# A decoder layer with a mixture of experts: another split of the last scatters, other load and result orders, paired overflow products and an earlier mask

## What is computed

```python
logits = x @ gate_weight.T;  scores = softmax(logits)
# the 3 best of 8 groups of experts, then the 6 best experts of 64 for every token
pos  = cumsum(one_hot(expert)) * one_hot - 1
slot = expert * C + minimum(pos, C - 1)            # C = 96 slots per expert
buf  = zeros(E * C, H).at[slot].set(x[tok])
out  = silu(buf @ Wg.T) * (buf @ Wu.T) @ Wd.T      # per expert, M = 176
y    = sum(out[slot] * topk_w)
shared = silu(x @ Sg.T) * (x @ Su.T) @ Sd.T
return y + shared
```

## Time and profile before

| what | value |
|---|---|
| median of 3 runs | 699.98 us (697.43 to 700.79) |
| the profiled execution | 692.44 us |
| its span | 690.4 us, mean granted clock 0.987 |
| PE busy | 637.3 us, 92% |
| DVE busy | 471.1 us, 68% |
| POOL busy | 345.6 us, 50% |
| ACT busy | 331.7 us, 48% |
| attention and gate | to about 398 us |
| shared groups 0 to 3, list | 398 to 452 us |
| experts | 452 to 642 us |
| the rest | 642 to 690.4 us |

### The profile page before, as it was taken

The page is one execution under the profiler, slowest core; times in us unless marked ns, Lnnn a source line. Parts: engine busy times, 40 slices in busy tenths (PEclk is TensorE's granted clock), DMA queues, the critical chain, the costliest instruction groups (busy, mean ns, idle before and its releaser), DMA issues. The chain is left out here.

```text
span 690.4 us, 16774 instructions
## 1 busy us (share of the span) xinstructions
PE 637.3 (92%) x6161; PEld 449.1 (65%) x6161; DVE 471.1 (68%) x1278; ACT 331.7 (48%) x630; POOL 345.6 (50%) x381
## 2 busy tenths in 40 slices
PE   3799999999879889999999999999999999999892
PEld 1366666666657667666776455577786778677652
DVE  1477777768779689999896689745554555455656
ACT  2577778777656776777665543122222222222010
POOL 5511322212543345254322346757787777787493
PEclk9999999999999999999999999999999999999997
DMA  8234333355452321432131189159999999944697
GB/s 262 37 64 95 85 62 71 88 110 112 110 118 34 81 68 24 92 81 57 29 103 39 54 220 253 38 142 242 261 259 262 252 247 263 238 77 63 153 356 258
DMA packets 144145, 94.27 MB, mean 137 GB/s; under 512 B 61552, under 2 KB 141680, under 8 KB 144064
## 3 DMA queue, kind: packets, MB, share of 16 engines
q1 hardware_dynamic: 129008, 74.58, 41.3%
q0 software_dynamic: 10400, 14.33, 11.4%
q10 hardware_dynamic: 4656, 4.29, 1.9%
HBM read 60.26 MB, written 24.50 MB: 123 GB/s over the span
## 5 line engine op out<-in xcount | busy, mean ns | idle before, releaser
L1559 POOL DMA_INDIRECT sum_d<-outs,targets x64 | 93.3, 1458 | 27.4 <-issue 14.2
L850 DVE TENSOR_REDUCE mx<-Sc 128x16 f32<-128x1024 f32 x64 | 78.2, 1222 | 27.4 <-PE Sc L455 27.2
L1378 PE MATMUL Sc<-xT,wgu_sb 128*128 128x96 f32 (+1 forms) x768 | 92.8, 271 | 0.0
L1378 PEld LDWEIGHTS Sc<-xT,wgu_sb 128*128 128x128 f32 (+1 forms) x768 | 87.2, 187 | 0.4 <-issue 0.4
L483 PEld LDWEIGHTS O<-vbd,ET 128*64 128x64 f32 x2048 | 66.6, 138 | 28.8 <-issue 16.9
L854 DVE TENSOR_TENSOR E<-Sc,mx 128x1024 f32<-128x1024 f32 x64 | 78.4, 1225 | 6.5
L706 ACT COPY ET<-ring 128x512 f32<-128x512 f32 x128 | 68.9, 590 | 28.1 <-PE ring L467 25.4
L745 ACT ACTIVATE E<-E 128x1024 f32<-128x1024 f32 x64 | 67.7, 1058 | 22.6 <-DVE E L854 22.4
L483 PE MATMUL O<-vbd,ET 128*64 128x34 f32 x2048 | 73.6, 225 | 4.3 <-ACT ET L706 3.8
L467 PE MATMUL ring<-ident,E 128*128 128x128 f32 x512 | 70.7, 280 | 5.6 <-ACT kT L660 5.4
L455 PE MATMUL Sc<-kbd,qT 64*64 64x256 f32 x1024 | 72.0, 384 | 3.8 <-DMA kbd<-kT 3.8
(11 more groups left out here) (212 smaller groups left out, 1210.1 us busy)
## 6 DMA issues: line engine op xcount, KB each, us to landing
wgu_sb<-in_wgu_dram SPq DMA_DIRECT2D x128, 176.0 KB, 3.7
sum_d<-zeros SPq DMA_DIRECT2D x16, 524.0 KB, 5.8
kbd<-kT SPq DMA_DIRECT2D x248, 32.0 KB, 2.2
wgu_sb<-sum_d SPq DMA_DIRECT2D x12, 512.0 KB, 9.3
wda_sb<-in_wd_dram SPq DMA_DIRECT2D x32, 160.0 KB
X<-in_x_dram SPq DMA_DIRECT2D x8, 512.0 KB, 6.8
rows_d<-xhT SPq DMA_DIRECT2D x8, 512.0 KB, 3.1
out_dram<-X ACTq DMA_DIRECT2D x8, 512.0 KB, 4.8
```

The costliest lines, as they stand in the source:

```text
L850: nc.vector.reduce_max(mx[:, m % 2, :], sc, AX.X).then_inc(s_mx, 1)
L1378: last = nc.tensor.matmul(GP[e % 2][0:m, CAP * u:CAP * (u + 1)], wgu_cols[j][:, c, m0:m0 + m], xT[:, e % 2, c, :], start=c == 0, stop=c == 1)
L1559: pool.indirect_dma_start(w["sums"][e % 2], bass.IndirectOffsetOnAxis(ap=targets[:, e:e + 1], axis=0), outs[:, e % OB, :], None, compute_o ...
```

## The change

It has five parts.

1. The scatters of experts 62 and 63 both go to table 1 (`table(e)`, `EVEN` = 62). Each waits for all earlier ones of its table (`ahead`).
2. SP loads all eight groups of table 0 first, as soon as the scatters of that table have landed and 62 gate-and-up products are done, and then those of table 1. The buffers are laid out so that table 0's lie in `xnT` and in the first weights' memory. The groups come in the order 0, 4, 1, 5, 2, 6, 3, 7 (`ORDER`), for adds, results and stores too. The two loads of `lastsb` go from SP's queue to ACT's.
3. The overflow products come in pairs, blocks j and j + 8 together: product by product one on the upper and one on the lower half of the partitions, in two banks. VectorE adds both banks. Results stand between the pairs and between the up pieces of group 7.
4. The mask is made at the list's time. `tk` gets memory of its own, which `outs` uses later. Its iota is written before the first `add`.
5. TensorE transposes `tokf` between the two halves of group 2's down products, and GpSimd holds the last third of `hidden(3)` back until `tokf` is there.

```diff
@@ moe_phase @@
+    def table(e):
+        return e % 2 if e < EVEN else 1
+    def ahead(e):
+        return sum(table(d) == table(e) for d in range(e))
+    in_table = [sum(table(e) == k for e in range(NE)) for k in range(2)]
...
-    tk = xnT[:, 1, 0:NT * 64]
+    tk = mem["tk"]
@@ sync @@
-            for j in range(OB):
-                sp.wait_ge(s_l[j], 16 * (NE // OB))
-            for h in range(2):
-                sp.dma_start(lastsb[NE * h:NE * (h + 1), :], w["lasts"]).then_inc(s_last, 16)
+            sp.wait_ge(s_gu, EVEN)
+            sp.wait_ge(s_dn, 2 * GE)
+            sp.wait_ge(s_s[0], 16 * in_table[0])
+            for g in ORDER:
+                sp.dma_start(y0[g], sums[0][g]).then_inc(s_y[g], 16)
             sp.wait_ge(s_gu, NE)
             sp.wait_ge(s_d, NE // 2)
...
+            sp.wait_ge(s_s[1], 16 * in_table[1])
+            for g in ORDER:
                 sp.dma_start(y1[g], sums[1][g]).then_inc(s_y[g], 16)
@@ tensor @@
+            early_up(GE - 1)
+            early_down(GE - 2, (0,))
             pe.wait_ge(s_sil, silus(GE - 1, 0))
             pe.wait_ge(s_tok, 7)
             nc.tensor.transpose(P[0][0:CAP, 0:NE], tokf[NE:128, :], ident[NE:128, NE:128]).then_inc(s_tt, 1)
+            early_down(GE - 2, (1,))
             early_down(GE - 1)
...
+            def overflow(j):
+                if 2 * j + 2 > OVER:
+                    pe.wait_ge(s_xo, 2 * j + 2 - OVER)
                 for t in range(2):
+                    at = 256 * j + 128 * t
+                    for i in range(2):
+                        rows = weight_rows(NG + j // 2 + NG // 2 * i)
+                        last = nc.tensor.matmul(P[(2 * j + i) % OVER][:, E * t:E * (t + 1)], wt[rows, at:at + 128],
+                                                lastsb[rows, :], start=True, stop=True)
                 last.then_inc(s_ov, 1)
@@ gpsimd @@
+                    if g == GE - 1 and c == 2:
+                        pool.wait_ge(s_tok, 7)
...
-                    pool.wait_ge(s_s[e % 2], 16 * (e // 2))
-                pool.indirect_dma_start(w["sums"][e % 2],
+                    pool.wait_ge(s_s[table(e)], 16 * ahead(e))
+                pool.indirect_dma_start(w["sums"][table(e)],
...
             last_token()
+            nc.gpsimd.iota(tk[:], pattern=[[-UNIT, NT * 64]], base=NT * 128 * UNIT, channel_multiplier=0,
+                           allow_small_or_imprecise_dtypes=True).then_inc(s_tk, 1)
             add(0)
@@ vector @@
             down_added(GS, 1)
+            dve.wait_ge(s_thr, 2)
+            dve.wait_ge(s_tk, 1)
+            nc.vector.scalar_tensor_tensor(out=wt[:], in0=tk[:], scalar=thr[:], in1=wt[:], op0=ALU.is_lt,
+                                           op1=ALU.mult).then_inc(s_over, 1)
...
             for k in BEHIND[1]:
                 late_drain(k)
+                if LATE[k][2] % 2 == 1 and LATE[k][2] > 1:
+                    result(ORDER[LATE[k][2] // 2 - 1])
+            for j in range(NG // 2, NG - 1):
+                overflow(j)
+                result(ORDER[j - NG // 2 + 2])
+            overflow(NG - 1)
             for k in BEHIND[2]:
                 late_drain(k)
+            for g in ORDER[5:]:
                 result(g)
```

More of the change, by code:

```diff
@@ L41 @@
 OB = 8
+EVEN = NE - 2
+ORDER = (0, 4, 1, 5, 2, 6, 3, 7)
 XB = 6
@@ L1330, in early_up, with early_down @@
                     up(g, u, P[u]).then_inc(s_up, 1)
-            def early_down(g):
-                for b in range(2):
+            def early_down(g, halves=range(2)):
+                for b in halves:
                     if 1 <= g <= GS:
@@ L1395, in down_pair @@
                 last.then_inc(s_d, 1)
-            for g in range(1, GE):
+            for g in range(1, GE - 1):
                 early_up(g)
                 early_down(g - 1)
+            early_up(GE - 1)
+            early_down(GE - 2, (0,))
             pe.wait_ge(s_sil, silus(GE - 1, 0))
@@ L1412, in _ @@
                     down_pair((e - 3) // 2)
-            def overflow(b):
-                if b >= OVER:
-                    pe.wait_ge(s_xo, b - OVER + 1)
+            def overflow(j):
+                if 2 * j + 2 > OVER:
+                    pe.wait_ge(s_xo, 2 * j + 2 - OVER)
                 for t in range(2):
-                    at = 256 * (b % NG) + 128 * t
-                    rows = weight_rows(NG + b // 2)
-                    last = nc.tensor.matmul(P[b % OVER][:, E * t:E * (t + 1)], wt[rows, at:at + 128], lastsb[rows, :],
-                                            start=True, stop=True)
+                    at = 256 * j + 128 * t
[3 more added lines that the diff above has]
+                                                lastsb[rows, :], start=True, stop=True)
                 last.then_inc(s_ov, 1)
@@ L1429, in _ @@
             pe.wait_ge(s_o, NE)
-            for b in range(NG):
-                overflow(b)
+            for j in range(NG // 2):
+                overflow(j)
             for k in BEHIND[1]:
                 late(k)
-            for b in range(NG, 2 * NG):
-                overflow(b)
+            for j in range(NG // 2, NG):
+                overflow(j)
             for k in BEHIND[2]:
@@ L1495, in _ @@
                     silu(e - 1)
+            for j in range(OB):
+                act.wait_ge(s_l[j], 16 * (NE // OB))
+            for h in range(2):
+                act.dma_start(lastsb[NE * h:NE * (h + 1), :], w["lasts"]).then_inc(s_last, 16)
             for pieces in BEHIND:
@@ L1498, in _ @@
                     late_silu(k)
-            for g in range(NG):
-                act.wait_ge(s_res, g + 1)
+            for i, g in enumerate(ORDER):
+                act.wait_ge(s_res, i + 1)
                 act.dma_start(out_rows[g], X[:, GT * g:GT * (g + 1), :]).then_inc(s_out, 16)
@@ L1748, in _, with overflow @@
                     late_drain(at_slot(e))
-            def overflow(b):
-                g = b // 2
-                dve.wait_ge(s_ov, b + 1)
-                if GE <= g < NG - 1:
-                    dve.wait_ge(s_ladd, GT * (g - GE + 1))
-                xt = X[:, 2 * b:2 * b + 2, :]
-                nc.vector.tensor_tensor(xt, P[b % OVER][:].rearrange("p (t e) -> p t e", e=E), xt,
-                                        ALU.add).then_inc(s_xo, 1)
+            def overflow(j):
+                dve.wait_ge(s_ov, j + 1)
+                for i in range(2):
+                    b = j + NG * i
+                    g = b // 2
+                    if GE <= g < NG - 1:
+                        dve.wait_ge(s_ladd, GT * (g - GE + 1))
+                    xt = X[:, 2 * b:2 * b + 2, :]
+                    nc.vector.tensor_tensor(xt, P[(2 * j + i) % OVER][:].rearrange("p (t e) -> p t e", e=E), xt,
+                                            ALU.add).then_inc(s_xo, 1)
             def result(g):
-                dve.wait_ge(s_sum, g + 1)
-                dve.wait_ge(s_xo, 2 * g + 2)
+                dve.wait_ge(s_sum, ORDER.index(g) + 1)
+                dve.wait_ge(s_xo, 4 * (g % (NG // 2)) + 4)
                 if g == NG - 1:
```

39 lines of the change are left out of this document (8 added, 31 removed).

## The result

| | before | after |
|---|---|---|
| median of the runs | 696.92 us (20 runs) | 700.27 us (20 runs) |
| lowest and highest | 690.67 to 700.79 | 696.22 to 706.00 |
| ratio, 95% interval | | 1.0063 (1.0041 to 1.0085) |
| profiled execution, its span | 692.44, 690.4 | 704.97, 703.0 |
| mean granted clock of it | 0.987 | 0.968 |

The change makes the kernel slower by 0.63%, some 4.4 us (the two medians lie 3.4 us apart). The forecast of 702.2 lies close to the median of after, but partly by luck: it stood on a median of 699.98 for before, which 20 runs put at 696.92, and on a difference of 2.2 us, half of the measured one. The one error made the forecast too high, the other too low; with 696.92 the same sum gives 699.1. The prediction counted up to 0.5% as no change. The measured 0.63% lies beyond that, the way of rival A, though its interval takes in 0.5%.

What follows compares the result with a forecast made beforehand. TensorE bounds the kernel until the experts end, then loads, adds and results. 0.8 us off the start, first add 4.4 us later at 660.2, last result 687.9: span 2.2 us more, 699.98 + 2.2 = 702.2 us, range 694 to 707.

Steps and rivals of the forecast that it cites:

- rival A: Odd table or clock makes the tail slower: up to 7.2 us over before; chance with rival C 0.22.
- The list: Start of the experts: earlier token transpose takes 0.8 us off, bounds 0 and 1.2 us.
- The mask: Its 2.34 us move to the list's time at cost 0; gain at the old place not in the sum.
- The first even load: SP's queue at the experts' end: first even table load goes out at 642.0, 5.7 us earlier.
- rival C: Another wait holds the even loads until 647 us: 7.2 us slower; chance together with rival A 0.22.
- The scatters, 4.1 us apart: Experts 61, 62 and 63 queue on one table at 640.4, 644.5 and 648.6, landed at 652.7.
- The first add, which needs the ninth load: GpSimd after the experts: 17.0 us after the first issue, first add at 660.2, 4.4 us later than before.
- The pairs: Overflow products: a pair costs 0.9 to 2.0 us; late products start some 3 us earlier, gain ending at the first result.
- The turns: Tail: GpSimd's adds and VectorE's results alternate by whole instruction, 2.2 us a queued add, 1.1 us a queued result.
- Rival B: Loads were the bound, turns cost little: 5.7 us less; chance 0.25 together with larger gains at the start.
- The end: Tail: last down pieces emptied at 684.3, three results to 687.9, last store 4.7 us later, span 692.6 us.
- The total: Whole kernel: span 2.2 us more than 690.4, time 702.2 us; first add between 654.5 and 661.5 given 0.53.

Runs made afterwards that it cites:

- kernel 9: Before with only the token transpose between the halves of group 2's down products and the last third of hidden(3) held behind the list; 696.14 us, ratio 0.9994.
- kernel 6: Before with the list, iota and mask edits alone; scatters, loads, overflow products and results as before; 693.45 us, ratio 0.9957.
- kernel 4: After, but SP waits for the scatters of both tables before the first load; 707.55 us, ratio 1.0172.
- kernel 1: After with experts 62 and 63 scattered to their old tables again, the even table's eight loads still first; 700.28 us, ratio 1.0068.
- kernel 2: As kernel 1, but loads go group by group from both tables, in the new order of groups; 695.12 us, ratio 0.9991.
- run 11: After with each overflow pair's products ordered both of one half of the rows, then both of the other; 700.05 us in one execution.
- run 3: After plus 30 unread filler products on TensorE, 18 before the last overflow pair, 12 between the last down pieces; 699.25 us, ratio 1.0061.
- kernel 5: After with only three even loads ahead, then three odd ones, then by pairs; 697.72 us, ratio 1.0017.
- kernel 8: As kernel 5, with the filler products of run 3 added; 699.00 us, ratio 1.0044.

## Why the prediction was right or wrong

- **The list.** Right in kind, low in size: 0.8 us taken, 1.1 measured, inside the bounds. That it "should reach the experts' end whole" holds for TensorE. The step that failed is the next one, which took the scatters and loads to move along with TensorE: scatter 60 began 2.3 us before the experts' end in before's profile and 0.1 us before it in after's. The first gather is 2.6 us earlier in list time (3.5 in place of 6.1), the last gather 0.5 us later (188.3 in place of 187.8). GpSimd's full stream had swallowed it. Each of these distances is from one profile per kernel.
- **The mask.** It holds up gathers where it stands now, as the prediction took it (2.15 us for one gather), and that costs nothing there, since the first scatter waits 3.9 us for VectorE anyway. Its old place was costed at nothing in the sum; the ratios of kernels 9 and 6 (0.9994 and 0.9957) suggest that this was too little, with intervals that overlap.
- **The first even load.** Forecast 1.6 us after the experts' end, measured 3.3: GpSimd's lag again. It did begin ahead, so rival C did not come.
- **The scatters, 4.1 us apart.** This is the term that failed most. Alone they are (4.06 and 4.02 us in kernel 4), among eight loads they take 4.66, 7.92 and 5.5. The odd table was complete 19.7 us after the experts' end, forecast 12.3. The rule weighed in rival A, that queues take turns packet by packet (Trainium skill, DMA: Bandwidth & Descriptors, Arbitration), does not protect a scatter here. The other figure of rival A, 5.97 us from rows 10, was misread. Before both scatters there GpSimd was idle for only the 0.30 us of issue, so neither waited for another; one of the other table lies between them, at 504.56. The 5.97 us are twice GpSimd's 2.98 us for each expert, its pace and not the time that a scatter takes among weight loads.
- **The first add, which needs the ninth load.** The mechanism was right and decides the sign: forecast 19.8 us after the experts' end, measured 23.6. Kernels 1 and 2 show it as the loss. Its 17.0 us from the first load are 17.4 in kernel 1 and 17.3 in kernel 4, where no scatter stands among the loads.
- **The pairs.** Forecast 0.9 to 2.0 us each, measured 0.9 to 1.0; that the gain ends at the first result was right. By the Trainium skill (TensorE: Matmul & The Clock Gate, The mechanism) products on different row groups of the array run at the same time and weight loads are pulled ahead; the trace agrees (four pairs in 3.7 us, in either order of run 11).
- **The turns.** Right: eight adds in 23.4 us (forecast 23.2) with no wait for a load, results of 2.17 us. Rival B did not come.
- **The end.** Forecast 27.7 us from the first add to the last result at full clock, measured 30.0. The clock fell in a pause of TensorE, as rival A said, but first in another one: in the 9.88 us ahead of the last overflow pair, where rival A saw 6.4 us between the last down pieces. It was 0.50 from 676 to 684 us, above 0.8 from 684 to 689, and 0.50 again from 689, behind the pause of 3.75 us between those pieces. 2.6 us of the tail are its (run 3). In the medians it is not seen.
- **The total.** From the experts' end to the last result the profile has 53.6 us for a forecast of 47.5: 3.8 of the difference is the first add, the other 2.3 lie in the tail, where run 3 gives the clock 2.6. Rival A priced both at 7.2 us over before and gave as its mark a first add after 661.5, 21.1 us after the experts' end; it came at 23.6. By the profile the loss from the list on is 8.0 us (253.9 - 246.0 to the last result), by the ratio of the runs 4.4. The sum was made against one execution of before that was 4.5 us under its median, with a high clock and few waits for scatters; the waits lie in the very stretch that I used as the standard.

## What to carry to other kernels

Starting transfers earlier gains nothing by itself: ask which transfer the first consumer needs, and count how many stand ahead of it. An engine whose instructions follow one another at their issue gap (0.30 us here) is a pace of its own even where the chain of waits runs through another engine; a head start given to the other does not reach what hangs on this one. And a single profiled execution is one draw: before its distances become the standard, set its time beside the median.

## What the runs showed of the hardware

- An accumulating scatter of 96 rows lands after 3.4 us alone, and takes 4.7 to 7.9 us until the next of its table starts or the table is complete when eight loads of 0.5 MB are queued; with three loads it takes 4.9 and 5.0 in kernel 5, 4.2 and 6.7 in kernel 8.
- VectorE's operation with two SBUF inputs (the mask, 2.34 us) holds up the indirect DMA that GpSimd issues beside it: a gather takes 2.15 or 2.16 us in place of 0.92 in all twelve kernels with the mask at the list, a scatter 2.66 (kernel 9) or 2.77 us (before) in place of 1.40. By the Trainium skill (SBUF — State Buffer, Who interferes with whom) two SBUF inputs hold up a GpSimd instruction that reads SBUF, not one that only writes it. These instructions write descriptors, which the prediction took to be free of it, but they also read row numbers (`tokens`, `targets`), and no run tells which of the two was held.
- Keeping TensorE at 2.4 GHz with filler products shortened its last piece from 5.49 to 2.86 us and changed neither median by more than its interval.
